# Second attention of a two-layer transformer: the rounded maxima are subtracted by TensorE in the score banks

## The reference, cut to what matters

```python
sc = jnp.einsum('bhnid,bhnjd->bhnij', Qb, Kw) / np.sqrt(D)
sc = jnp.where(mask[None, None], sc, -jnp.inf)
p = jax.nn.softmax(sc, axis=-1)
out = jnp.einsum('bhnij,bhnjd->bhnid', p, Vw)
...
lsc = jnp.where(lmask[None, None], lsc, -jnp.inf)
lp = jax.nn.softmax(lsc, axis=-1)
rem = jnp.einsum('bhsn,bhnd->bhsd', lp, GV)
...
out = gl * local + gr * rem          # gl, gr: sigmoids of Q against two gate vectors
```

## Time and profile before

| | us |
|---|---|
| median of 3 runs (lowest, highest) | 1734.24 (1732.9, 1735.41) |
| the profiled execution, its own time | 1731.67 |
| its span, first to last instruction | 1729.7 |

### The profile page before, as it was taken

One profiled execution on the slowest core, in us unless ns is written; L12 is line 12 of the kernel. 1 busy time (PEld: TensorE's weight loads), 2 busy tenths in 40 slices (PEclk: granted clock), 3 DMA queues, 4 the chain that ended last, 5 costly groups with the idle time before them and its releaser, 6 DMA issues. The chain is left out here.

```text
span 1729.7 us, 44740 instructions
## 1 busy us (share of the span) xinstructions
PE 1519.1 (88%) x14049; PEld 1113.3 (64%) x14051; DVE 1121.4 (65%) x2643; ACT 999.0 (58%) x2526; POOL 932.2 (54%) x1633
## 2 busy tenths in 40 slices
PE   4798999999999999998999688888888888885785
PEld 4654555555555555554999577777777777774674
DVE  3346555555555555553556398989989899886662
ACT  4344555555555555554334388888888888872333
POOL 6333555555555555455454366666666666642665
PEclk8579999999999999999999699999999999996766
DMA  7403222222222121122333112112121121215442
GB/s 197 135 13 71 57 56 56 56 56 56 56 56 52 48 54 53 51 54 67 85 69 67 37 42 47 43 41 44 43 46 42 43 46 43 42 41 115 85 85 41
DMA packets 240803, 103.37 MB, mean 60 GB/s; under 512 B 145449, under 2 KB 229226, under 8 KB 240746
## 3 DMA queue, kind: packets, MB, share of 16 engines
q1 hardware_dynamic: 230506, 89.04, 21.8%
q0 software_dynamic: 10240, 13.64, 3.7%
HBM read 57.73 MB, written 35.96 MB: 54 GB/s over the span
## 5 line engine op out<-in xcount | busy, mean ns | idle before, releaser
L669 POOL TENSOR_SCALAR_AFFINE_SELECT probs<-probs 128x512 f32<-128x512 f32 x256 | 184.3, 744 | 164.5 <-ACT probs L1548 164.5
L976 DVE TENSOR_REDUCE mneg<-bankS 128x2 f32<-128x256 f32 x256 | 107.3, 419 | 224.4 <-PE bankS L1886 224.2
L1548 ACT ACTIVATE probs<-bankT 128x1024 f32<-128x1024 f32 x128 | 131.1, 1024 | 188.5 <-PE bankT L1899 188.5
L977 DVE TENSOR_REDUCE mneg<-bankS 128x2 f32<-128x512 f32 x256 | 174.4, 681 | 0.0
L1543 ACT ACTIVATE qT<-bankA,bd 128x256 f32<-128x256 f32 x256 | 107.6, 473 | 94.4 <-PE bankA L1868 94.4
L1868 PE MATMUL bankA<-xnT,wd 128*128 128x256 f32 x512 | 150.5, 418 | 0.0
L662 POOL CAST qb<-qT 128x256 bf16<-128x256 f32 x256 | 97.8, 401 | 95.8 <-ACT qT L1543 95.7
L1896 PE MATMUL bankT<-qT,kT 37*128 37x512 f32 x512 | 140.1, 624 | 7.1 <-DMA qT<-mT 5.2
L1336 DVE STREAM_TRANSPOSE pt<-pe 128x768 f32<-128x768 f32 x128 | 124.4, 972 | 25.4 <-ACT pe L1649 25.3
L1913 PE MATMUL bankB<-probs,vaug 128*64 128x512 f32 x512 | 139.9, 625 | 1.1 <-ACT yT L1555 1.0
L1555 ACT COPY yT<-bankB 128x512 f32<-128x512 f32 x128 | 75.1, 586 | 83.7 <-PE bankB L1917 83.7
(11 more groups left out here) (317 smaller groups left out, 4322.5 us busy)
## 6 DMA issues: line engine op xcount, KB each, us to landing
rzb<-reciprocals SPq DMA_DIRECT2D x128, 128.0 KB
yT<-yT SPq DMA_DIRECT2D x64, 128.0 KB
xtab<-tab SPq DMA_DIRECT2D x32, 192.0 KB, 2.0
xs_sorted<-zeros SPq DMA_DIRECT2D x1, 4608.0 KB, 18.8
qT<-xs_sorted SPq DMA_DIRECT2D x144, 32.0 KB, 1.8
ys_sorted<-qT SPq DMA_DIRECT2D x36, 128.0 KB, 1.9
value_rows<-vrow SPq DMA_DIRECT2D x32, 128.0 KB, 1.8
vx<-value_rows SPq DMA_DIRECT2D x256, 16.0 KB, 1.8
```

What stands on the lines that cost most here:

```text
L669: pool.affine_select(out=blocks, in_=blocks, compare_op=ALU.is_ge, fill=0.0, base=0, pattern=[[0, 4], [1, P]], channel_multiplier=-1).then ...
L976: dve.tensor_reduce(mneg[:, n.half, :, j, 0], bankS[:, :, 0:128], AX.X, ALU.max, negate=True)
L977: dve.tensor_reduce(mneg[:, n.half, :, j, 1], bankS[:, :, 128:384], AX.X, ALU.max, negate=True).then_inc(S["red_done"], 1)
L1548: act.activation(pT[:, g % 2].rearrange("p e j t -> p e (j t)"), bankT[:, 0:2, :], ACT.Exp, scale=SCALE0).then_inc(S["exp_done"], 1)
```

## The change

DVE keeps only the maxima; they are written negated and rounded to bf16 (`mxn`, by `top` in place of `shift`). A new PE call `subtract(b, g)` adds them onto the scores in place: an identity matrix times the negated maxima, each repeated over its 64 columns, one product of 384 columns for each of the two banks. ACT takes the exponentials from the banks, one of 384 numbers for each bank, in place of one of 768 from SBUF. A bank is therefore held until its exponentials are taken: `scores(b, g)` for g of 2 and 3 and `gate(b)` wait for `exp2` where they waited for `sub_done`. In PE's order the four `subtract` calls are put in, and `gate(b)` moves from before `attend(b, 0)` to behind `attend(b, 1)`; `count(n)`, which stood between these two attends, now follows `gate(b)`. ACT's order of calls, POOL's and SP's are not touched.

```diff
-            def shift(b, g):
+            def top(b, g):
                 k = g % 2
                 s = (bankS, bankT)[k][:, 0:2, 0:6 * NL].rearrange("p b (g k) -> p b g k", k=NL)
                 dve.wait_ge(S["s2_ps"], b.b * 4 + (g + 1))
-                dve.tensor_reduce(mxs[:, k, :].rearrange("p (b g) -> p b g", b=2), s, AX.X, ALU.max).then_inc(S["red2"], 1)
-                dve.wait_ge(S["red2"], b.b * 4 + (g + 1))
-                if g >= 2:
-                    dve.wait_ge(S["exp2"], b.b * 4 + (g - 1))
-                dve.tensor_tensor(pr[:, k, :].rearrange("p (b g k) -> p b g k", b=2, k=NL), s,
-                                  mxs[:, k, :].rearrange("p (b g) -> p b g", b=2).unsqueeze(3).to_broadcast([P, 2, 6, NL]),
-                                  ALU.subtract).then_inc(S["sub_done"], 1)
+                dve.tensor_reduce(mxn[:, k, :].rearrange("p (b g) -> p b g", b=2), s, AX.X, ALU.max, negate=True).then_inc(S["red2"], 1)
...
-                act.activation(pe1[:, g % 2].rearrange("p k s q -> p s k q"), pr[:, g % 2, :].rearrange("p (s k q) -> p s k q", k=2, q=W),
-                               ACT.Exp, scale=SCALE1).then_inc(S["exp2"], 1)
+                s = (bankS, bankT)[g % 2][:, 0:2, 0:6 * NL]
+                for c in range(2):
+                    ins = act.activation(pe1[:, g % 2, :, 6 * c:6 * c + 6, :].rearrange("p k s q -> p s k q"),
+                                         s[:, c].rearrange("p (s k q) -> p s k q", k=2, q=W), ACT.Exp, scale=SCALE1)
+                ins.then_inc(S["exp2"], 1)
...
                 if g >= 2:
-                    pe.wait_ge(S["sub_done"], b.b * 4 + (g - 1))
+                    pe.wait_ge(S["exp2"], b.b * 4 + (g - 1))
...
+            def subtract(b, g):
+                k = g % 2
+                pe.wait_ge(S["red2"], b.b * 4 + (g + 1))
+                for c in range(2):
+                    ins = pe.matmul((bankS, bankT)[k][:, c, 0:6 * NL], identb[:, :], mxn[:, k, 6 * c:6 * c + 6].unsqueeze(2).to_broadcast([P, 6, NL]),
+                                    start=False, stop=True, skip_group_check=True)
+                ins.then_inc(S["sub_done"], 1)
...
             def gate(b):
...
-                pe.wait_ge(S["sub_done"], b.b * 4 + 3)
+                pe.wait_ge(S["exp2"], b.b * 4 + 3)
...
                 if b:
+                    subtract(b, 1)
                     scores(b, 2)
...
                 if b:
+                    subtract(b, 2)
                     scores(b, 3)
                 if n:
                     values(n)
                 if b:
+                    attend(b, 0, n is None)
+                    subtract(b, 3)
+                    attend(b, 1, n is None)
                     gate(b)
-                    attend(b, 0, n is None)
                 if n:
                     count(n)
                 if b:
-                    attend(b, 1, n is None)
                     shared_up(b, n is None)
...
                 if n:
+                    subtract(n, 0)
                     scores(n, 1)
```

More of the change, by code:

```diff
@@ L230, in program @@
         wsum = sb("wsum", [P, 2, 2])
-        mxs = sb("mxs", [P, 2, 12])
-        pr = sb("pr", [P, 2, 12 * NL])
+        mxn = sb("mxn", [P, 2, 12], BF16)
         pe1 = sb("pe1", [P, 2, 2, 12, W])
@@ L1375, in step1 @@
                 if b:
-                    shift(b, 1)
+                    top(b, 1)
                 if p:
@@ L1380, in step1 @@
                     turn(b, 0)
-                    shift(b, 2)
+                    top(b, 2)
                 if p:
@@ L1388, in step1 @@
                 if b:
-                    shift(b, 3)
+                    top(b, 3)
                 if m:
@@ L1404, in step1 @@
                 if n:
-                    shift(n, 0)
+                    top(n, 0)
                 if b:
```

## The result

The changed kernel takes 1801.04 us (median of 4 runs, 1798.6 to 1802.05), the kernel before 1734.83 beside it (1732.9 to 1740.58). The ratio is 1.0385, 95% interval 1.0359 to 1.0410: slower by 66 us. 1781 was predicted, with a range of 1764 to 1803. The profiled execution has a span of 1798.9 us, 69.2 more than before.

What follows compares the result with a forecast made beforehand. No engine was full; a ring of waits of 18.16 us a step bounded the kernel. Late gate 1.40 plus exponentials 0.12, over 31 steps, gave 47.1 us: 1778.8, with 2.57 to the median 1781 us; range 1764 to 1803.

Steps and rivals of the forecast that it cites:

- The ring: Chain of waits from one ACT `qs` to the next, 18.16 us a step; DVE's four subtractions are off it.
- The late gate: `gate` behind `attend(b, 1)` makes ACT wait 1.40 us before the gates' tanh: +1.40 us a step.
- A: The start of PE's `attend(b, 0)`, at 1234.30 in the rows of the step read.
- A stays: Added PE work ahead of `attend(b, 0)` fits in 1.71 us of idle time, so ACT still sets its start.
- The exponentials in two: ACT's pairs of 384 for one of 768: +0.06 each, +0.12 us a step, bounds 0.02 and 0.24.
- The rest of the ring: Taken unchanged; PE free at T + 5.67 ahead of `remote` at T + 5.97, a slack of 0.30.
- T: The start of DVE's transpose of group 3.
- Rival 3: PE gets to `remote` late and a second ring closes: 0.5 us a step more, 1797 us; chance 0.09.
- The sum: 1.40 + 0.12 = 1.52 us a step, 47.1 us over 31 steps.
- the own case: The prediction's main case, slower by the late gate and split exponentials: 1781 us; chance 0.80.
- Rival 1: DVE sets the pace after all; the kernel gets faster by 1.16 to 2.76 us a step, 1649 to 1698; chance 0.07.
- Rival 2: No change, if `attend(b, 0)` starts 1.4 us earlier: 1732 to 1737 us; chance 0.04.

Runs made afterwards that it cites:

- Experiment 2: The changed kernel with the gate products ahead of `attend(b, 1)`, still behind the third subtraction: 1782.55 us, ratio 1.0305.
- experiments 5 to 7: Changed kernel with gate in free banks: 1752.99 us; also third subtraction ahead of `attend(b, 0)`: 1748.87; then key copies on DVE, third subtraction behind `attend(b, 1)`: 1732.06.
- experiment 8: The kernel before, DVE still subtracting, with ACT's four key copies moved to DVE: 1752.59 us, ratio 1.0113.
- experiment 6: The changed kernel with the gate in free bank halves and the third subtraction ahead of `attend(b, 0)`: 1748.87 us, ratio 1.0085.
- experiment 1: The kernel before with only the gate moved behind the second attend, `count` following it; DVE still subtracts: 1814.66 us, ratio 1.0484.

## Why the prediction was right, and where its sizes were off

- **The ring and the idle DVE** held: 111 us of DVE's work went and no step became shorter. DVE waits before the transpose of group 3 for 3.14 us in the first of the steps shown, over the 2.5 that were named.
- **The late gate** was the right mechanism. ACT waits before the tanh in every step, for PE's gate product. The term from A to the tanh was undersized: 2.83 predicted, 3.21 measured. Its four parts, predicted and measured: `attend(b, 0)` 0.65 and 0.75, `subtract(b, 3)` 0.34 and 0.43, `attend(b, 1)` 0.77 and 0.86, gate with lag 1.07 and 1.17. Each is 0.09 to 0.10 too short, because each duration was taken from a neighbour of like kind. In the new order PE changes between attends (64 columns of weights) and products on 128 columns at each of these places. The trace of before had the price: from `attend(b, 3)` at 1238.61 to the masks at 1239.48 (line below) it is 0.87, from attend to attend 0.77. Experiment 2 shows that the change is what was missed: where the gate stands right behind the subtraction, with no change between them, the two take 0.34 and, with the lag, 1.06, as worked out. In all, +0.38 a step.
- **A stays** held for one step in two. A is 7.18 or 7.37 us behind `qs` in turn, in both kernels: 7.18 is the step of the prediction, and in the next one before, ACT's last latent copy ended PE's idle time at 1.89 in place of 1.71 (line below). There the later A moved the denominators by 0.09 (12.56 behind `qs`, 12.47 in the step of the rows), the `qk` behind them took 0.86 to the next group in place of 0.97, and the two steps are 18.17 and 18.16. Now PE's way from A is the ring, and it counts: +0.1 in the mean.
- **The exponentials in two** were oversized: +0.12 predicted, nothing found. A pair has 0.85 to 0.88, but the next instruction starts 0.75 behind the start of the pair (1236.33 to 1237.08), where it was 0.74 behind that of the single one (1230.49 to 1231.23, line below). From `qs` to the end of the last latent copy ACT takes 7.13 in both kernels. The Trainium skill (ScalarE: Activation LUTs, What ACT_TABLE_LOAD costs) would have a pair of 384 at 0.09 more than one of 768; the runs show 0.01, with the pair read from PSUM and the single one from SBUF, two effects that they do not separate.
- **The rest of the ring** held: tanh to denominators 3.88 for 3.86, denominators to `qs` 5.62 in place of 5.69. PE came to `remote` free 5.77 us behind T, where 5.67 was worked out, and still waited for DVE (0.24). Rival 3, the second ring, did not close, but it is at its limit: the idle time of ACT ahead of `qs`, which was counted as a reserve (0.42, 15.1 us in 31 waits before), is gone in all steps but one.
- **The sum** at full clock: 1.40 + 0.38 + 0.10, nothing for the exponentials, less 0.05 from the last part, is 1.83 a step for the 1.52 that was predicted: 57 us, not 47.
- **The clock** is what the prediction left out. It held it at 1.00 without a word. It took PE's gate out of PE's wait and filled the wait only in part, and did not ask what the idle time does to the granted clock. Nine long steps cost 12.7 us by the trace, and filling the idle time gave back 10 to 12.5. Without this term the time would have been some 1788.
- **The range** held by luck in part. What was worked out for the own case ended at 1798; 1803 came from widening it for rival 3, and 1801 is nearer to that rival's 1797 than to 1781. The place that was kept for a second ring was filled by the clock.
- **Rival 1** fell by experiments 5 to 7: even with the gate out of the way DVE's relief gains nothing over before. By the rule of the Trainium skill (Perfetto Trace Analysis, Identifying the Most-Contended Engine) DVE was the engine to relieve; it had 16.3 of 18.0 us busy and was still not the one that was waited for. In experiment 8, at 18.1 of 19.1, it is.
- **Rival 2** asked for an earlier A, and nothing in the change gave one.

The lines of before that are named above, of PE and of ACT, with ACT's last latent copy and the denominators of the second step:

```profile
1239.48 0.34 PE L2077 MATMUL bankS<-masks,pick 64*128 64x384 bf16 x2
...
1252.64 0.34 PE L2161 MATMUL bankT<-vx,pt 128*64 128x68 f32 x4 [1.89 <-ACT gkm L1692]
```

```profile
1231.23 0.73 ACT L1687 COPY gvx<-bankT 32x32 f32<-32x32 f32 x4
...
1233.42 0.83 ACT L1692 COPY gkm<-bankT 32x64 f32<-32x64 f32 x4
...
1257.84 0.20 ACT L1733 COPY dens<-bankT 128x48 f32<-128x48 f32 x1 [1.66 <-PE bankT L2166]
```

Left open: why every third step falls to the lower clock and not each one, since the idle stretches are alike in the steps beside it (and why only three fell in experiment 2); what holds A by 0.19 in every second batch; and what the 14 us are made of that experiment 6 still has over before, beyond the late count and A in the step shown.

## What to carry to other kernels

Relieving the busiest engine gains nothing if the ring of waits does not pass its work; ask first which engine the moved work lands on, and what then stands between the start of that ring and the instruction that the next engine waits for. A buffer that is held longer can be dearer than the work that was saved: here the scores' bank, kept until the exponentials, pushed the gate behind the first attend, PE's order pushed it behind the subtraction and the second, and putting the gate into another bank took back most of the loss. When work leaves an engine's idle time, the hole it leaves is part of the change: look at what the clock does behind it.

## What the runs showed of the hardware

- The granted clock of a step fell to 0.92 (3.18 us of it at 0.50, the 1.2 GHz level) behind PE's idle stretches of 0.66 and then 1.19 or 1.38 us, in nine of 30 steps; in the 21 others, with stretches of the same lengths, it stayed at 1.00 (0.97 in the first). It fell in 29 of 30 steps with one stretch of 2.6 to 2.7 us ahead of the first attend (experiment 1). With 1.71 to 1.89 us there (before) it stayed at 1.00. Products that nothing uses, put into the stretches, kept it at 1.00 and made both kernels faster, by 10 to 12.5 and by about 41 us.
- Changing between attends on 64 columns of weights and products on 128 costs PE about 0.1 us each time: 0.86 to 0.87 from an attend to the next group in place of 0.77.
- Two products of 384 bf16 columns on all 128 rows took 0.34 to the next group on 128 by 128 weights (experiment 2) and 0.43 to an attend, where the pair of masks on 64 rows each is followed after 0.17 by products that are on 64 rows as well.
